# Cross-attention on one NeuronCore: scores and the loop's projections as 64-row tiles, outputs two batches behind

## What is computed

```python
Q = query @ Wq.T + bq            # (8, 112, 256), 16 heads of 16
K = key_value @ Wk.T + bk        # (8, 375, 256)
V = key_value @ Wv.T + bv
scores = einsum('bhqd,bhkd->bhqk', Q, K) / sqrt(16)
attn = softmax(scores, axis=-1)
context = einsum('bhqk,bhkd->bhqd', attn, V)
x = context @ W_o.T + b_o + query
out = (x - mean(x)) / sqrt(var(x) + 1e-5) * gamma + beta
```

## Time and profile before

| | us |
|---|---|
| median of 3 runs | 156.63 (154.4 to 158.67) |
| the profiled execution | 157.02 |
| its span, first to last instruction | 155.2 |
| TensorE matmuls busy | 134.0 (86%) |
| TensorE weight loads busy (beside the matmuls) | 116.7 (75%) |
| VectorE busy | 105.6 (68%) |
| ScalarE busy | 80.4 (52%) |
| POOL busy | 60.7 (39%) |
| before the loop's first unit | 32.9 |
| batches 0 to 7 of the loop begin at | 32.9, 51.9, 67.8, 82.7, 97.6, 112.6, 123.8, 135.8 |

### The profile page before, as it was taken

One profiled execution on the slowest core, in us unless ns is written; L12 is line 12 of the kernel. 1 busy time (PEld: TensorE's weight loads), 2 busy tenths in 40 slices (PEclk: granted clock), 3 DMA queues, 4 the chain that ended last, 5 costly groups with the idle time before them and its releaser, 6 DMA issues.

```text
span 155.2 us, 3853 instructions
## 1 busy us (share of the span) xinstructions
PE 134.0 (86%) x1466; PEld 116.7 (75%) x1466; DVE 105.6 (68%) x247; ACT 80.4 (52%) x163; POOL 60.7 (39%) x83
## 2 busy tenths in 40 slices
PE   5799989679979999889998998999899996779850
PEld 4599779468768899769988987899787875667620
DVE  6745997757937769947896699578779887031252
ACT  3648437214426666526655666465656565566410
POOL 8946997920003998404140504130023023041051
PEclk9999999987999999999999999999999999999997
DMA  4976989698950250697414050405031001001002
GB/s 128 358 259 216 269 296 227 159 270 239 301 204 2 102 156 0 169 267 235 135 52 151 4 178 4 155 2 183 24 128 34 4 4 30 4 4 30 4 0 59
DMA packets 14354, 19.58 MB, mean 126 GB/s; under 512 B 2192, under 2 KB 13520, under 8 KB 14336
## 3 DMA queue, kind: packets, MB, share of 16 engines
q1 hardware_dynamic: 13056, 17.26, 35.6%
q0 software_dynamic: 592, 1.70, 4.5%
q10 hardware_dynamic: 688, 0.38, 0.8%
HBM read 6.30 MB, written 0.92 MB: 47 GB/s over the span
## 4 chain that ended last, share of the span: by engine, by line
PE 65%; DVE 11%; DMA 10%; ACT 6%; issue 5%; SPq 1%; POOLq 0%; ACTq 0%; DVEq 0%
PE m_bank L793 19%; PE pv_bank L873 12%; PE st_bank L857 11%; PE mx_bank L834 10%; DMA q_stack<-shift 6%; DVE mx L656 6%; PE m_bank L901 4%; DMA c_raw<-ctxT 3%; PE m_bank L884 2%; ACT pw L561 2%; PE st_bank L793 2%; DMA q_stack<-q_first 1%; DVE q_hl L618 1%; PE m_bank L841 1%; ACT o_normT L552 1%
## 5 line engine op out<-in xcount | busy, mean ns | idle before, releaser
L656 DVE TENSOR_REDUCE mx<-mx_bank 112x1 f32<-112x375 f32 x128 | 64.6, 541 | 20.4 <-PE mx_bank L834 19.8
L561 ACT ACTIVATE pw<-st_bank 125x448 f32<-125x448 f32 x90 | 48.5, 548 | 48.5 <-PE st_bank L857 47.7
L834 PE MATMUL mx_bank<-k_stack,q_stack 128*112 128x376 f32 x128 | 41.3, 351 | 2.2 <-DVE mx L656 1.2
L857 PE MATMUL st_bank<-q_stack,k_stack 128*125 128x224 f32 x180 | 37.7, 294 | 1.7 <-DMA q_stack<-shift 1.7
L857 PEld LDWEIGHTS st_bank<-q_stack,k_stack 128*125 128x125 f32 x180 | 30.0, 190 | 5.5 <-issue 3.0
L834 PEld LDWEIGHTS mx_bank<-k_stack,q_stack 128*112 128x112 f32 x128 | 22.0, 181 | 4.5 <-DVE mx L656 2.4
L359 POOL TENSOR_TENSOR c_hl<-c_raw,c_hl 128x752 fp32r<-128x752 f32 x6 | 10.9, 1814 | 27.5 <-DVE c_hl L612 27.5
L873 PE MATMUL pv_bank<-pw,v_sb 125*17 125x112 f32 x720 | 20.4, 260 | 1.1 <-ACT o_raw L535 1.1
L405 POOL TENSOR_SCALAR var_eps<-mv 112x1 f32<-112x1 f32 x7 | 1.6, 223 | 49.2 <-DVE mv L692 49.2
L793 PE MATMUL m_bank<-c_hl,w_hl 128*128 128x376 f32 x84 | 18.7, 365 | 0.9 <-ACT w_hl L449 0.9
L873 PEld LDWEIGHTS pv_bank<-pw,v_sb 125*17 125x17 f32 x720 | 16.3, 97 | 3.9 <-issue 2.2
(11 more groups left out here) (102 smaller groups left out, 160.6 us busy)
## 6 DMA issues: line engine op xcount, KB each, us to landing
k_stack<-k_hl SPq DMA_DIRECT2D x48, 188.0 KB, 2.5
c_raw<-ctxT SPq DMA_DIRECT2D x8, 375.0 KB, 4.3
q_stack<-q_hl SPq DMA_DIRECT2D x6, 224.0 KB, 4.5
q_stack<-q_hl SPq DMA_DIRECT2D x6, 168.0 KB, 3.4
x_space<-x_nat POOLq DMA_DIRECT2D x1, 896.0 KB, 10.3
out<-yo SPq DMA_DIRECT2D x8, 112.0 KB, 1.9
pw<-wT SPq DMA_DIRECT2D x2, 256.0 KB, 4.8
x_space<-xT SPq DMA_DIRECT2D x1, 448.0 KB, 6.1
```

What stands on the lines that cost most here:

```text
L561: nc.scalar.activation(p_tile[0:KC, n % PR, :, :], st_of(n)[0:KC, 0:4 * Q].rearrange("p (j q) -> p j q", j=4), ACT.Exp, scale=float(DK) ** ...
L656: nc.vector.tensor_reduce(mx[b % 2][:, h % 2, q_pair(h // 2):q_pair(h // 2) + 1], mx_bank[n % MR][0:Q, 0:KV], axis=AX_X, op=ALU.max, negat ...
L834: nc.tensor.matmul(mx_bank[n % MR][0:Q, 0:KVP], q_stack[k][:, side, q_pair(h // 2), b - Q_STACKS[k][0], :], k_stack[b % 3][:, h // 2, :], ...
L857: last = nc.tensor.matmul(st_of(n)[0:KC, k * 2 * Q:(k + 1) * 2 * Q], k_stack[i % 3][:, 2 * g + k, c * KC:(c + 1) * KC], q_stack[qk][:, :, ...
```

## The change

- **Scores for maxima and shifted scores** of batches 1 to 7 are matmuls over 64 rows, those of one side. The Q stacks of these batches have no zeros and one copy (`[PART, NP, n, Q]` instead of `[PART, 2, NP, n, Q]`), filled by three DMAs of 128 source rows in place of six of 64. Batch 0 keeps its stack; its shifted scores read 64 rows of it, its scores for maxima 128.
- **A unit** is now one side's four heads of half the pairs by 125 keys: four matmuls of 64 rows, 125 stationary and 112 moving columns, in one bank. Units alternate between the sides, beginning with side 1. The first head for the maximum in a unit stands behind the first of the four. Value products come for half a batch at a time, once its six units are done.
- **K and V of batches 3 to 7** are made by `k_rows` and `v_rows`: each 128-row half of the contraction is two tiles of 64 rows, one writing each of two banks, issued in turn. Both tiles need all input channels, so a copy of the context with the two 64-row halves exchanged (`c_swap`, two DMAs a batch on SP's queue, `swap_context`) and one of the weights (`w_swap`, eight DMAs on POOL's queue) are added. K is done in units 3, 4, 5 (6, 7, 8 in batch 0), V in 9, 10, 11 (later in batches 0 and 1).
- **K's split** for those batches: ScalarE copies K with its bias to `k_full` (`take_k`), VectorE rounds it (`round_k`), POOL subtracts (`subtract_k`).
- **First shift in halves**: batch 0's first eight maxima are transposed and sent by themselves, the rest in unit 1 of the loop. Ahead of the loop stand 14 heads (20 before); batches 0 and 1 take 20 and 22, the later ones 16 each. V of batch 2 moves into units 1 to 3, Q of batches 5 to 7 to units 4 and 5.
- **Outputs**: the transposition of the normalised output goes into the bank and visit of a later batch's maxima; the output projections of batches 0 to 2 run at unit 1 of batches 3 to 5, that of 3 and 4 in batch 5 also, 5 in batch 6, 6 in batch 7. The scaling of z by its mean and deviation moves from VectorE to POOL.
- The context's high part is cast on ScalarE for all batches.

```diff
@@ TensorE: scores @@
-                nc.tensor.matmul(mx_bank[n % MR][0:Q, 0:KVP],
-                                 q_stack[k][:, side, q_pair(h // 2), b - Q_STACKS[k][0], :],
-                                 k_stack[b % 3][:, h // 2, :], start=True, stop=True).then_inc(max_full, 1)
+                rows = slice(64 * side, 64 * side + 64) if b >= 1 else slice(0, PART)
+                q = (q_stack[0][rows, side, q_pair(h // 2), 0, :] if b == 0 else
+                     q_stack[k][rows, q_pair(h // 2), b - Q_STACKS[k][0], :])
+                nc.tensor.matmul(mx_bank[n % MR][0:Q, 0:KVP], q, k_stack[b % 3][rows, h // 2, :],
+                                 start=True, stop=True).then_inc(max_full, 1)
...
-                for k in range(2):
-                    last = nc.tensor.matmul(st_of(n)[0:KC, k * 2 * Q:(k + 1) * 2 * Q],
-                                            k_stack[i % 3][:, 2 * g + k, c * KC:(c + 1) * KC],
-                                            q_stack[qk][:, :, q_pair(2 * g + k), i - Q_STACKS[qk][0], :], start=True, stop=True)
+                rows = slice(64 * side, 64 * side + 64)
+                for p in range(HP):
+                    a = HP * half + p
...
+                    last = nc.tensor.matmul(st_of(n)[0:KC, p * Q:(p + 1) * Q],
+                                            k_stack[i % 3][rows, a, c * KC:(c + 1) * KC], q, start=True, stop=True)
+                    if p == 0:
+                        for h in heads:
+                            scores_for_max(h)
@@ TensorE: projections of batches 3 to 7 @@
+            def row_tiles(dst, lhs, rhs, product, first, last):
+                a, c = PRODUCTS[product]
+                for swapped in range(2):
+                    for e in range(EC):
+                        done = [nc.tensor.matmul(dst[t], lhs(t, a, e, swapped), rhs(t, c, e, swapped),
+                                                 start=(first and swapped + e == 0),
+                                                 stop=(last and swapped + e == EC)) for t in range(2)]
+                return done
@@ SP, POOL: copies with the 64-row halves exchanged @@
+                for to, at in ((0, 64), (64, 0)):
+                    sp.dma_start(c_swap[b % 2][to:to + 64, :, :, :].bitcast(F32),
+                                 c_hl[b % 2][at:at + 64, :, :, :].bitcast(F32)).then_inc(c_swapped[b % 2], 16)
...
+            for part in range(2):
+                for to, at, k in ((0, 64, D), (64, 0, D + PART)):
+                    pool.dma_start(w_swap[to:to + 64, part, :, 0:PART].bitcast(F32),
+                                   w_hl[part][at:at + 64, :, k:k + PART].bitcast(F32)).then_inc(w_swapped, 16)
+                    pool.dma_start(w_swap[to:to + 64, part, :, PART:PART + D].bitcast(F32),
+                                   w_hl[part][at:at + 64, :, 2 * D:3 * D].bitcast(F32)).then_inc(w_swapped, 16)
@@ order @@
-EARLY_HEADS = H + 4
+EARLY_HEADS = 14
+HEADS = (1, 1, 3, 1, 1, 1, 1, 1, 3, 1, 1, 1)
+FIRST_HEADS = ((2, 1, 2, 2, 2, 2, 2, 2, 2, 1, 1, 1), (2, 2, 2, 2, 2, 1, 2, 1, 2, 2, 2, 2))
+V_UNITS = ((11, 11, 11), (10, 11, 11), (9, 10, 11))
+NORM_WITH = {3: 0, 4: 1, 5: 2, 6: 4, 7: 5}
+U_MT = (11, 9, X2, X2, X2, X2, 6)
```

More of the change, by code:

```diff
@@ L319, in _ @@
                 stack_k(1, t)
-            for side in range(2):
-                stack_q(sp, 1, side)
-            for t in range(2):
-                stack_k(2, t)
+            stack_q(sp, 1)
+            stack_k(2, 0)
+            swap_context(3)
+            stack_k(2, 1)
             load_context(4)
@@ L461, in q_hi_part @@
                 if k == 2:
-                    for side in range(2):
-                        act.wait_ge(q_in[1][side], 48)
+                    act.wait_ge(q_in[1][0], 48)
                 n = Q_STACKS[k][1] - Q_STACKS[k][0]
@@ L703, in take_bv @@
                 last.then_inc(bv_ready, 1)
-            for n in range(H):
+            for n in range(EARLY_HEADS):
                 head_max(n)
@@ L757, in _ @@
             normalise_half(1)
-            scale_to_norm(B - 2)
             b = B - 1
@@ new lines, in context_rows, with weight_rows, k_rows @@
+            def context_rows(b, t, part, e, swapped, at):
+                return (c_swap if swapped else c_hl)[b % 2][64 * t:64 * t + 64, part, e, at]
+            def weight_rows(t, part, e, swapped, at):
+                rows = slice(64 * t, 64 * t + 64)
+                if swapped:
+                    return w_swap[rows, part, e, at]
+                first = D + PART * t if at.start < PART else 2 * D - PART
+                return w_hl[part][rows, e, first + at.start:first + at.stop]
+            def k_rows(b, product):
+                if product == 0:
+                    for t in range(2):
+                        claim("K", b, t)
+                    pe.wait_ge(c_swapped[b % 2], 32 * ((b - AHEAD) // 2 + 1))
+                    pe.wait_ge(w_swapped, 128)
+                banks = [m_bank[m_job("K", b, t)[0]] for t in range(2)]
+                done = row_tiles([bank[:, 0:KVP] for bank in banks],
+                                 lambda t, part, e, swapped: weight_rows(t, part, e, swapped, slice(0, PART)),
+                                 lambda t, part, e, swapped: context_rows(b, t, part, e, swapped, slice(0, KVP)),
+                                 product, product == 0, product == 2)
+                if product == 2:
+                    for t in range(2):
+                        done[t].then_inc(m_full[m_job("K", b, t)[0]], 1)
@@ L1002, in _ @@
-                    for n in heads[1:]:
-                        scores_for_max(n)
+                    if i + AHEAD < B:
+                        first = FIRST_K if i == 0 else U_K
+                        if u in range(first, first + 3):
+                            k_rows(i + AHEAD, u - first)
+                        for piece in range(3):
+                            if u == V_UNITS[min(i, 2)][piece]:
+                                v_rows(i + AHEAD, piece)
+                    for h in heads[1:]:
+                        scores_for_max(h)
```

566 lines of the change are left out of this document (348 added, 218 removed).

## The result

The changed kernel takes 191.0 us (median of four runs, 189.0 to 192.3) where the kernel before takes 156.2 (four runs, 154.4 to 158.7). The ratio is 1.223, with an interval of 1.205 to 1.242. I had forecast 150, with a range of 142 to 157.5. The sign was wrong, and the size lies beyond even the dearest rival of 175. The profiled execution is the slowest of the four, 192.3 at a mean granted clock of 0.83; the other three had 0.84 to 0.87.

A forecast was written before the change was run, and what follows sets the result against it. TensorE was taken to bound the middle batches, VectorE batch 5. From the profiled 157.0 us, -1.7 - 0.2 - 1.9 - 2.2 + 1.0 - 1.4 = -6.4 gave 150.6, in round figures 150 for the median; range 142 to 157.5.

The forecast's parts named there:

- Other changes of tile size stay as many, at some 0.19: Whole loop: beyond the shared output transposes (-0.1), the number of tile-size changes stays the same, each some 0.19 us.
- the front, -1.9: Ahead of the loop: with the first shift halved, the loop starts at 31.0, between ends of 28.4 and 34.5; -1.9 us.
- Shifted scores: TensorE's units: loads of the two sides overlap, three loads a unit show, 0.31 us; scores gain 1.2 a middle batch.
- V: V projection in a middle batch: 24 pairs, 12 at 0.12 and 12 at 0.11 us, 2.75 in all, a loss of 0.6.
- Rival (3): TensorE's scores and projections: loads follow one another whatever the side, slower than before, 175 us; chance 0.15.
- (2): Units: next unit's first load not fetched early, 0.42 us a unit; 156, or 159 us; chance 0.20 including a late K chain.
- Rival (1): Units: 64-row loads hidden altogether, 0.2 us a unit, 1.3 less in each of batches 0 to 4; 143.5 us; chance 0.15.
- Batch 2: Third batch of the loop: no output projection yet, 0.8 more gained than in batches 3 and 4; -1.9 us, to 13.0.
- Batches 3 and 4: Middle batches: scores -1.2, K +0.05, V +0.6, outputs -0.6 and -0.1, new waits 0.15; -1.1 us each, to 13.9.
- Batch 1: Second batch: six heads more +1.0, same-side heads +0.6, steady gain 1.1, wait for shifts covered 0.67; -0.2 us.
- Batch 5: Three layer norms in place of one: VectorE work 11.5 us, over 0.9 busy, batch length 12.2, +1.0.
- Batch 0: First batch: V(2) +2.1, bias product -0.9, scores -0.7, V +0.6, idle won back -0.9; +0.2 us.

The follow-up runs named there:

- the filled kernel with the projection ahead: Changed kernel with 24 unread matmuls in TensorE's wait ahead of the loop, output projection ahead of value products in batches 3 to 5: 177.4, again 181.9 us (178.1 to 190.0).
- the first blocks: Kernel before plus unread blocks ahead of the loop, 60 whole matmuls of 112 columns between blocks: pairs and whole matmuls of 112 columns 0.21 us apart at half clock.
- The filled kernels: Changed kernel with 24 unread matmuls in the wait ahead of the loop: 181.0 us; with output projection also ahead of value products: 177.4, then 181.9.
- the blocks: Unread matmul blocks, one form each, ahead of the kernel before's loop; at full clock, a height change cost 0.19 us with 376 columns, 0.13 with 112.
- the kernel with the projection ahead: Changed kernel with the output projection ahead of unit 1's value products in batches 3 to 5: 187.9 us, batches 3 and 4 at 15.6 each.
- the second kernel of blocks: Kernel before plus unread blocks ahead of the loop, separated by 24 whole matmuls of 376 columns: whole matmul of 112 columns 0.109 us, pair 0.110.

## Why the prediction was wrong

**The steps that failed** are two: a term that the sum doesn't have, the granted clock, and the sentence "Other changes of tile size stay as many, at some 0.19".

**The clock** is the larger. The change empties TensorE's queue for 5.06 us ahead of the loop, which I saw only as "the front, -1.9". In the kernel before, showed the waits there and the earlier trace rows the 0.91 of batch 0: the sign that a wait at this place costs clock was in the rows, and I asked what an earlier start was worth, but not what the engine would do until then. The clock fell at 30.2, within that wait, and was back at 57.5; the kernel before has it down for 3.4 us. Of the profiled 190.4 us, 17% of the clock was not granted, against 2% of 155.2 before: 32 and 3 us, if all of that time were TensorE's pace. It is less, as batch 0 has 3.6 us of other idle time. An estimate from the filled kernel with the projection ahead, 177.4 less the 9 us of clock that it lacks (0.053 of 175.6), gives 168 at the full clock, 12 over the kernel before. So the larger part of the 35 us that the change cost, over 20 by this estimate, is the clock.

What keeps the clock down behind the wait is shown only in part. In the kernel before with the maxima alone in 64 rows it stayed down for 22 us of batch 0, where without the changes of height it needed 3.4. In the changed kernel batch 0 has fewer changes, and many matmuls of 112 columns, which in the first blocks stood at half the clock for 100 us, for the most part with no change of height near them; no run separates the two. Why the clock falls again in batches 5 to 7 is open. It isn't the number of changes: 7 to 10 a batch there, and 24 in batch 5 of the kernel with the maxima alone, at the full clock. The filled kernels had a higher clock in this stretch (0.84 to 0.98 in three profiles, against 0.73 and 0.78 in two without the filling), but differ among themselves about as much.

**The changes of tile size.** I had a price from the way to the 32-column tiles and back, 0.19 for both ways, and then counted only the changes that were there. Before, no matmul of 64 rows existed; after, I counted 14 changes of height along the trace of batch 0, 7 in batch 1, 4 in each of batches 2 to 4, and 7, 10 and 9 in the last three, 59 in all. Some take the place of changes of width at the value products, which the kernel before had as well, 4 a batch. Height and width counted together, the traces have 36 changes before and 76 after: 13 more in batch 0, 1 or 2 more in each of batches 2 to 4, 2 to 6 in the others. For batches 2 to 4 the sentence was nearly right. The 40 more are 5 to 8 us at the 0.13 to 0.19 of the blocks, an estimate, and more at half the clock; I had priced none of them.

**Shifted scores** (0.31 a unit with a head) and **K** (0.7 a product) were right; **V** at 0.103 to 0.12 was right. Rival (3), loads one after another, is refuted, and so is (2), no look-ahead, as long as no other height comes between. Rival (1) had 0.2 a unit with a head, and 0.28 to 0.33 speaks against it.

**Batch 2**: 14.2, forecast 13.0. **Batches 3 and 4**: 16.2 and 15.8, forecast 13.9. Part is the four changes at the value products, which are dearer now: the last two matmuls of a unit take 0.31 ahead of the value products (100.99 to 101.30), where two take 0.11 elsewhere. The greater part is waits between TensorE and VectorE, which I had put at 0.15: in the kernel with the projection ahead they are 1.2 us still (0.35, 0.21, 0.64). While TensorE does 2.3 us of values and projection in one piece it issues no head, VectorE has nothing, and then VectorE's piece of layer norm and subtractions makes TensorE wait. Mean busy shares (11.6 of 16.2 for VectorE) don't show this; the order of the two queues does.

**Batch 1**: forecast 15.7, at the full clock 17.6 (in the filled kernel with the projection ahead, timed again). Five more changes of tile size and a wait of 1.2 for the maxima's low part stand in it. **Batch 5**: forecast 12.2 with VectorE busy over 0.9. At the full clock it took 14.4 with VectorE at 10.5. The amount of its work was right (forecast 11.5, so a little high), but it was not the bound: there too the two wait for one another. **Batch 6**: 11.4 at the full clock, forecast 10.5.

**Batch 0**: forecast 19.2, of which 1 idle. With the front filled it took 29.2. The mean clock of 0.88 makes 3.5 of that; six waits (1.63 for the second shifts, 1.51 for the maxima's low part, 0.89, 0.79, 0.55, 0.45) make 5.8, 4.8 more than forecast; and 13 more changes of tile size 1.7 to 2.5. That gives 29 to 30, so nothing large is left over. The halved shift moved its second wait into the batch, and I had no term for it.

**The outputs**: TensorE's wait of 0.59 is gone, as forecast; VectorE waits for the projection instead, 1.70. **The front**: 31.05, as forecast.

## What to carry to other kernels

Count how often TensorE changes its tile height or width, before and after, and price each: here 0.13 to 0.19 us in blocks. A tile that by itself costs nothing extra, or even halves the work, cost 30 us when it was put between whole matmuls, some 21 of them at the full clock. Group the tiles of one height, or leave all in one. And where an edit shortens a chain to an engine, ask what the engine does in the time gained: in a wait of 5 us the clock of this kernel fell, and it was down for 27. Filling that wait won 2 to 4 us up to batch 2. A larger gain in the total came from batches far behind it, and changed from run to run: look at where a gain lies before you put it down to the edit.

## What the runs showed of the hardware

- Weight loads of the two row halves run at one time: 240 matmuls of 64 rows in 13.2 us, as 120 of 128 rows in 13.1.
- What a load of 125 columns costs depends on the granted clock. Whole matmuls of 112 columns with such loads stand 0.109 apart at 2.4 GHz and 0.21 at 1.2. Whether the load itself takes twice as long or is no longer hidden, the distances don't tell. The Trainium skill, TensorE: Matmul & The Clock Gate, LDWEIGHTS, gives P/1.2 ns, 0.104 for 125 columns, as if it were one figure for both; the blocks at half the clock differ from it.
- Matmuls of different row halves don't always start in program order. In batch 6 of the changed kernel, at half the clock, the next unit's four (for the other half) start in step with the four ahead of them:

```profile
161.00 0.45 PE L1059 MATMUL st_bank<-q_stack,k_stack 64*125 64x112 f32 x1
161.01 0.45 PE L1059 MATMUL mx_bank<-q_stack,k_stack 64*125 64x112 f32 x1
161.25 0.41 PE L1059 MATMUL st_bank<-q_stack,k_stack 64*125 64x112 f32 x1
161.26 0.41 PE L1059 MATMUL mx_bank<-q_stack,k_stack 64*125 64x112 f32 x1
```

- A busy TensorE is no sign of a rising clock. For 100 us without a gap, matmuls of 112 columns, of either height and mixed, stayed at 1.2 GHz once a wait had put it there; in the second kernel of blocks the unmixed ones began with 2.4 GHz and kept it.
